# A Mamba block with a routed expert layer on one core: two of four channel groups' causal convolutions move from TensorE to ScalarE and GpSimd

## The reference

```python
xz = h @ W_in                                   # 256 -> 2*512
x_in, z = jnp.split(xz, 2, axis=-1)
x_c = jax.nn.silu(_causal_depthwise_conv(x_in, conv_w, conv_b))   # 512 channels, 4 taps
dbc = x_c @ W_xproj
dt, Bm, Cm = jnp.split(dbc, [DT_RANK, DT_RANK + D_STATE], axis=-1)
delta = jax.nn.softplus(dt @ W_dt + b_dt)
A = -jnp.exp(A_log)
y = _selective_scan(x_c, delta, A, Bm, Cm, D_param)   # s = exp(d_t*A)*s + d_t*B_t*u_t ; y_t = s . C_t
y = y * jax.nn.silu(z)
return y @ W_out
```

## Time and profile before

| | |
|---|---|
| three runs | 2338.16 us median (2337.91 to 2339.09) |
| profiled execution | 2337.82 us, its span 2336.3 us |
| PE busy | 2150.1 us, 92% |
| DVE busy | 2038.1 us, 87% |
| POOL busy | 1915.5 us, 82% |
| ACT busy | 1661.5 us, 71% |
| mean granted clock | 0.979 |

### The profile page before, as it was taken

One profiled execution on the slowest core, in us unless ns is written; L12 is line 12 of the kernel. 1 busy time (PEld: TensorE's weight loads), 2 busy tenths in 40 slices (PEclk: granted clock), 3 DMA queues, 4 the chain that ended last, 5 costly groups with the idle time before them and its releaser, 6 DMA issues. The chain is left out here.

```text
span 2336.3 us, 45628 instructions
## 1 busy us (share of the span) xinstructions
PE 2150.1 (92%) x13383; PEld 1731.7 (74%) x13383; DVE 2038.1 (87%) x2843; ACT 1661.5 (71%) x3402; POOL 1915.5 (82%) x1207
## 2 busy tenths in 40 slices
PE   8889899999999998989898989898987999999996
PEld 5667677767767777767677767676766899999885
DVE  5999999999999999899989999999999556647776
ACT  6686878778787878777778787878775444445664
POOL 3887989898988989888889898989898567667775
PEclk9999999999999999999999999999998999999998
DMA  6041414132232414050505141414134667668886
GB/s 188 2 154 46 146 52 149 65 127 92 100 115 77 146 55 170 21 171 21 171 21 173 38 155 51 140 61 140 56 127 155 142 117 158 140 95 160 182 182 153
DMA packets 226007, 263.60 MB, mean 113 GB/s; under 512 B 101123, under 2 KB 182563, under 8 KB 225636
## 3 DMA queue, kind: packets, MB, share of 16 engines
q1 hardware_dynamic: 175172, 208.07, 29.2%
q0 software_dynamic: 29904, 34.77, 8.3%
q10 hardware_dynamic: 20688, 17.85, 2.5%
HBM read 196.75 MB, written 71.71 MB: 115 GB/s over the span
## 5 line engine op out<-in xcount | busy, mean ns | idle before, releaser
L893 POOL TENSOR_TENSOR dbu<-drive_u,w_all 128x1024 f32<-128x1024 f32 x384 | 904.0, 2362 | 98.5 <-DVE ps_a L754 46.9
L1172 ACT ACTIVATE ps_a<-delta,a_neg 128x512 f32<-128x512 f32 x768 | 517.2, 685 | 140.0 <-DVE area L754 120.3
L910 POOL TENSOR_TENSOR wp<-area 128x1024 f32<-128x1024 f32 x192 | 453.0, 2359 | 37.5 <-DVE area L754 36.8
L766 DVE TENSOR_TENSOR wd<-ps_a,area 128x1024 f32<-128x1024 f32 x320 | 383.1, 1197 | 0.0
L1436 PEld LDWEIGHTS ps_y<-ident,wd 128*128 128x128 f32 x2560 | 301.3, 144 | 98.6 <-issue 70.8
L1436 PE MATMUL ps_y<-ident,wd 128*128 128x128 f32 x2560 | 338.8, 277 | 12.8 <-DVE wd L766 12.8
L2019 POOL DMA_INDIRECT acc_scratch<-ow,e_meta x135 | 220.9, 1636 | 133.1 <-DVE ow L1930 121.0
L1463 PEld LDWEIGHTS ps_a<-dg,duT 128*128 128x128 f32 x2048 | 252.8, 199 | 67.6 <-issue 66.6
L1463 PE MATMUL ps_a<-dg,duT 128*128 128x128 f32 x2048 | 263.6, 284 | 38.4 <-ACT carry L1179 35.9
L2261 PEld LDWEIGHTS e_ps_h<-xT,w_tile 128*128 128x128 f32 x2160 | 260.6, 192 | 16.2 <-DVE xT L1908 9.6
L2261 PE MATMUL e_ps_h<-xT,w_tile 128*128 128x128 f32 x2160 | 266.1, 277 | 2.1 <-DVE xT L1908 1.4
(11 more groups left out here) (245 smaller groups left out, 3772.9 us busy)
## 6 DMA issues: line engine op xcount, KB each, us to landing
area<-b_scratch SPq DMA_DIRECT2D x128, 512.0 KB, 5.0
w_all<-b_scratch SPq DMA_DIRECT2D x96, 512.0 KB, 4.2
dg<-xs_scratch SPq DMA_DIRECT2D x540, 32.0 KB
area<-in_L_attn_x_dram SPq DMA_DIRECT2D x32, 512.0 KB, 5.2
ee<-acc_scratch SPq DMA_DIRECT2D x32, 512.0 KB, 4.2
x_scratch<-area SPq DMA_DIRECT2D x16, 512.0 KB, 2.9
acc_scratch<-area SPq DMA_DIRECT2D x16, 512.0 KB
area<-x_scratch ACTq DMA_DIRECT2D x32, 256.0 KB
```

What stands on the lines that cost most here:

```text
L766: dve.tensor_tensor(wd[:, s % NWD], states(k, 2), cc[:, n:n + 2, :], ALU.mult).then_inc(wd_done, 1)
L893: pool.tensor_tensor(dbu[:, k % NBU], du[:, g % 2, :].unsqueeze(1).broadcast_to([P, 2, CH]), bb[:, row:row + 2, :], ALU.mult).then_inc(dbu ...
L910: pool.tensor_tensor(wp[:, s % 2], ss[:, s % 2], cc[:, rows, :], ALU.mult).then_inc(wp_done, 1)
L1172: act.activation(dst, dl[:, g, :], ACT.Exp, scale=a_neg[:, g, n:n + 1]).then_inc(exp_done, 1)
```

## The change

For groups 0 and 1 of every chunk but the first, the two `conv` uses leave `STEADY`. ScalarE instead makes four products (the tap's shifted rows of `xin`, times the tap's weight): the one of the last tap, with the bias, goes straight to `xc` (L1153 of the new kernel), the others in turn to the two halves of the area of `xb` (L1160). GpSimd adds them to `xc` one by one, in place (`add_tap`, L929).

```diff
-                  ("out", 1, -1, 16, 2, 6), ("x", 2, 1, 21, 1, 3), ("conv", 0, 1, 22, 1, 2), ("x", 3, 1, 23, 2, 2),
-                  ("conv", 1, 1, 23, 4, 6), ("dt", 3, 0, 27, 1, 3), ("conv", 2, 1, 27, 3, 5),
+                  ("out", 1, -1, 16, 2, 6), ("x", 2, 1, 21, 1, 3), ("x", 3, 1, 23, 2, 2),
+                  ("dt", 3, 0, 27, 1, 3), ("conv", 2, 1, 27, 3, 5),
...
+        OFF_PE = (0, 1)
+        TAPS_ACT = ((12, 13, 14, 16), (21, 22, 23, 27))
+        TAPS_ADD = ((7, 8, 9), (12, 13, 15))
...
+        tap_rows = xb[:].rearrange("p i d -> p (i d)").rearrange("p (k t) -> p k t", k=2)
...
+            def add_tap(q, j, k):
+                n = len(OFF_PE) * (q - 1) + j
+                pool.wait_ge(taps_made, TAPS * n + k + 2)
+                if k > 0:
+                    pool.wait_ge(taps_added, (TAPS - 1) * n + k)
+                u = xslot(q, OFF_PE[j])
+                pool.tensor_tensor(u, u, tap_rows[:, k % 2], ALU.add).then_inc(taps_added, 1)
...
+            def tap_product(q, j, k):
+                g = OFF_PE[j]
+                added = (TAPS - 1) * (len(OFF_PE) * (q - 1) + j)
+                scale = cw[:, g, k:k + 1]
+                rows = xin[:, g, k:k + CH]
+                if k == TAPS - 1:
+                    t = q * G + g
+                    if t >= 6:
+                        act.wait_ge(gated, t - 6)
+                        act.wait_ge(du_done, t - 5)
+                    act.wait_ge(*emptied("x", g, q))
+                    ins = act.activation(xslot(q, g), rows, ACT.Identity, bias=cb[:, g:g + 1], scale=scale)
+                else:
+                    if k == 0:
+                        act.wait_ge(norm_done, q + 1)
+                        act.wait_ge(taps_added, added)
+                    if k == 2:
+                        act.wait_ge(taps_added, added + 1)
+                    ins = act.activation(tap_rows[:, k % 2], rows, ACT.Copy, scale=scale)
+                ins.then_inc(taps_made, 1)
...
             def silu_u(q):
+                act.wait_ge(taps_added, (TAPS - 1) * len(OFF_PE) * q)
                 for g in range(G):
-                    act.wait_ge(*emptied("conv", g, q))
+                    if g not in OFF_PE:
+                        act.wait_ge(*emptied("conv", g, q))
...
+                for j, steps in enumerate(TAPS_ACT):
+                    if s in steps and c + 1 < NC:
+                        tap_product(c + 1, j, (3, 0, 1, 2)[steps.index(s)])
```

More of the change, by code:

```diff
@@ L310, in mamba_block @@
         e_done = sem("e_done")
+        taps_made = sem("taps_made")
+        taps_added = sem("taps_added")
         NW = 8
@@ L481, in load_x @@
                     sync.wait_ge(norm_done, q)
+                if q == 2:
+                    sync.wait_ge(taps_added, (TAPS - 1) * len(OFF_PE))
                 if q >= 3:
@@ L925, in _ @@
                     times_u(t + 1)
+                for j, steps in enumerate(TAPS_ADD):
+                    for k, offset in enumerate(steps):
+                        q = due(at, offset, 1, G * HB)
+                        if q:
+                            add_tap(q, j, k)
                 q = due(at, FACTOR, 2, G * HB)
@@ L1095, in empty @@
                         act.wait_ge(norm_done, min(q + 3, NC))
+                        act.wait_ge(taps_added, (TAPS - 1) * len(OFF_PE) * min(q + 2, NC - 1))
                         if q > 0:
```

## The result

| | before, beside it | after |
|---|---|---|
| median | 2338.24 us (2337.91 to 2339.09) | 2389.55 us (2384.38 to 2392.03) |
| profiled execution | 2337.82 us, its span 2336.3 us | 2392.03 us, its span 2390.1 us |
| PE / DVE busy | 2150.1 / 2038.1 us | 2108.3 / 2044.7 us |
| POOL / ACT busy | 1915.5 / 1661.5 us | 2025.5 / 1714.2 us |
| mean granted clock | 0.979 | 0.957 |

What follows compares the result with a forecast made beforehand. No engine is full; VectorE, doing the scans, sets the pace. Chunk 0's +0.7, seven even chunks at +0.5 and seven odd at -0.4 sum to +1.4 on 2337.82, 2339.2, taken as 2340 us; 8-in-10 range 2320 to 2358.

Steps and rivals of the forecast that it cites:

- the stalls of the earlier trace: t1, n = 8 to 11: VectorE's waits from group 0's convolution can go, 2.9 us a chunk, at most 44 us.
- ScalarE's products hidden: ScalarE, steps 14 to 20 and t1: eight products less two copies, +3.8 us a chunk, covered by idle time and waits.
- the price of an addition: GpSimd: 1.23 us from start to start for each of six adds, 7.4 us a chunk.
- the stand at the first one: Behind b7 of t0, even chunk: GpSimd stands 4.0 us for ScalarE's second product before group 0's first add.
- the gate and w2 in t1: Even chunk: w2 of t0 done at 958.0, before 952.5; gate of t1 starts at 959.15, 2.6 us late.
- t1 as a whole: Even chunk: 3.48 us of stalls gained against n = 4 2.9 us late; VectorE 0.6 us ahead at n = 12.
- In t2 it is given back: t2, even chunk: w1 done at 979.4 delays scan n = 0, which loses the 0.6 us gained in t1.
- n = 4 0.5 us late: t2, even chunk: scan n = 4 comes 0.5 us late, leaving the even chunk at +0.5 us.
- w2 done at 984.4, so the gate comes at 985.5: t2, even chunk: GpSimd ends w2 at 984.4, so the gate comes at 985.5 against 985.12.
- rival 3: TensorE's clock falls in the 4 us gap of t1: 0.5 to 1.5 us a chunk, 2347 to 2362; chance 0.18.
- Rival 2: GpSimd becomes the bound, lateness behind w2 of t1 not worked off before t0: 2353 to 2361; chance 0.22.
- Rival 1: The stalls in t1 go and the chain costs nothing: 2294, or 2316 if it costs half; chance 0.24.

Runs made afterwards that it cites:

- experiment 5: The changed kernel without GpSimd's adds, ScalarE still making all eight products: 2297.86 us, ratio 0.9823.
- experiment 7: The changed kernel with group 0's three additions one GpSimd step later and FACTOR_X1 moved from 17 to 15: 2349.24 us, ratio 1.0037.
- experiment 2: The changed kernel with group 0's three additions one GpSimd step later each, the first behind b0 of t1: 2335.96 us, ratio 0.9981.

## Why the prediction was wrong, point by point

**Right, with their sizes:** the stalls of the earlier trace rows and their cause (experiment 5: 2297.86, against 2294); ScalarE's products hidden (they take 0.81 and 0.72 us each, summed with 0.66 and 0.62 from start to start); the price of an addition (1.28 us on average, 1.23 from start to start); the stand at the first one (3.19 us idle; forecast 4.0 from the end of b7 of t0, which itself comes 0.6 us later than I reckoned); the gate and w2 in t1 within 0.3 us; and t1 as a whole, -0.7 against -0.6.

**The step that failed** is "In t2 it is given back", with its "w1 is done at 979.4. The scan n = 0 of t2 needs its buffer" and "n = 4 0.5 us late": 1.1 and 0.15 us a chunk were forecast, 6.0 and 4.4 measured. The time of w1 was right to 0.3 us. What failed was the list of who waits for GpSimd there:

- `turn_p` of w1. It stands at n = 15 in TensorE's order, and the prediction followed only w2's turn. Before, w1 was done 5.4 us ahead of it, at 972.99 for 978.37; the change took away this margin from both sides (w1 6 us later, TensorE without group 1's matmuls). I booked the matmuls that leave as a gain everywhere, and didn't ask what they covered at the place where they had stood.
- `x_ln`. It stands in GpSimd's order behind b1 of t2 as a copy's worth of time, so I counted its time and not its reader. Before, it was done 3.9 us ahead of its use (975.5 for 979.42). It comes 6.1 us later now (783.08, translated 981.6), and ScalarE, 0.7 us ahead by itself, stands for 2.86 us in front of two exps.
- "w2 done at 984.4, so the gate comes at 985.5" took TensorE to be idle when w2 comes. w2 of t1 ends at 785.5, translated 984.0, as forecast; its turn runs at 789.24, translated 987.8, because TensorE is still busy with what the gap and the clock held up.

To these comes a term that the sum put at nothing: TensorE's clock, which rival 3 looked for in t1 only. In t2 it makes the loss at n = 4 (0.5 to 2.3 us a chunk where it falls, 0.0 where it doesn't) and the one at n = 10, 13 us in all 16 chunks.

**The rivals.** Rival 3, TensorE's clock, had the mechanism right and the place wrong. It looked at the 4-us gap of t1; in t1 TensorE's gaps are 1.65 and 0.95 us, `turn_p` takes 1.09 us behind each, and the granted clock stays at 1.00 (windows 748.00 to 754.00 and 754.00 to 762.00). It is in t2 that the clock falls, at the gap of 3.30 us and again ahead of n = 10. The granted clock over the span is 0.957 for 0.979: at half speed that is some 2 x 0.043 x 2390 = 206 us at the low level, for 2 x 0.021 x 2336 = 98. By the Trainium skill ("TensorE: Matmul & The Clock Gate", Part 1) an idle TensorE falls to the lower clock; the trace agrees in t2, with 1.97 us for 1.04 behind the gap. But ahead of n = 10 it also fell when TensorE had been busy for 10.2 us without a break. That experiment 7 is slower than 2 by 13 us, and 32 us faster with four useless matmuls, is the plainest sign of what the clock costs. Rival 2 (GpSimd the bound) falls: it is idle for 17.8 us in two chunks, and t0 and t3 lose nothing. Rival 1 is what comes out when the additions are put elsewhere.

**What would have shown it** was in the prediction's own means: the end of w1 (979.4) beside the start of its turn in TensorE's timeline (978.37).

Left open: why the clock came back sooner in experiment 2 than in 7 after equal gaps, why it didn't fall at all in chunks 9 and 13 of the change, and why it falls ahead of n = 10 in some chunks only.

## What to carry to other kernels

When an engine's order gets later, list for each instruction behind the delay who waits for it and by how much it was ahead, the small ones (a 0.2-us factor) first; one that is put down by its duration alone is a hole in the sum. Work that is taken off an engine opens a gap where it stood: ask what comes next in that engine's order and whether its input is there by then. Where two late hand-overs end close together, mending one shows almost nothing (9 and 10 us alone, 31 together), so try them together before either is dropped; and move half of the work before all of it.

## What the runs showed of the hardware

At a gap of 3.30 us in TensorE its granted clock went from 1.00 to 0.50, for 6.8 us in all (779.76 to 786.59, so from 0.9 us ahead of the gap's end on): `turn_p` took 1.97 us for 1.04 and four pieces of convolution 3.62 for 1.88. In experiment 2 it was low for 3.4 us at a gap of 3.29. Gaps of 1.65 and 0.95 us in t1 had no such effect, nor one of 2.89 us ahead of a drive in t3 (819.08, 2.02 us for sixteen; 1.95 in t2), nor gaps of 3.18 and 3.17 us in chunks 9 and 13; and ahead of n = 10 the clock fell with gaps of 0.62 and 0.24 us or with none. So the length of a gap alone doesn't decide. Four unread matmuls of 128x512 in the gap, 3.7 us of TensorE's time, kept it at 1.00 and made the kernel 10 to 32 us faster. And a two-input fp32 addition of 128x512 on GpSimd took 1.28 us also while VectorE's scans ran beside it, the same as `times_u` before (1.275 us): no slowing by its neighbour was seen.
